# An embedding kernel's first image group: loaded and measured in two halves, weights scaled in between, GpSimd's table products held back

## The chip, the cores and the metric

The kernel runs on one core of a Trainium2 chip. The metric is the device time of one execution in microseconds (us); less is better. The engines of the core are called PE (matrix products), DVE (vector), ACT (scalar), POOL (GpSimd) and SP (the engine that here only issues transfers, "DMAs").

## The reference, cut to what matters

The model embeds 32 images and 32 texts and passes them through a scan layer and a mixture of experts. The change touches only the image embedding and, beside it, a set of tables for the scan layer:

```python
# x: (32, 3, 224, 224); P = 16, h = w = 14
x = transpose(x.reshape(B, C, h, P, w, P), (0, 2, 4, 3, 5, 1)).reshape(B, h*w, P*P*C)
x = layernorm(x, ln1_g, ln1_b)                 # over the 768 values of a patch
x = einsum('bnp,pd->bnd', x, W_proj) + b_proj  # 768 -> 192
x = layernorm(x, ln2_g, ln2_b)
x = concatenate([cls, x], axis=1) + pos_embedding
...
# scan layer: h = sigmoid(A) h + sigmoid(Bp) x_t,  y = sum over states of sigmoid(C) h
```

## The kernel before, in words

`embed_images` treats the 32 images as four groups of eight (`GB` = 8, `NGRP` = 4). One partition holds one row of patches of one image: 14 rows by 8 images make 112 partitions. `xg[g % 2]` is the tile of a whole group, [112, 48, 224]: 3 channels times 16 pixel rows (48), and 224 pixels. Two such tiles take turns, so groups 0 and 1 can be loaded at once, and groups 2 and 3 must wait until the tile is free. A group is worked on in 14 steps, one for each column of patches.

**The engines' parts.** DVE measures each patch (`x_stats`: two `bn_stats` of 384 values for a column, each over half of the 48 rows), then makes mean and deviation of all 14 columns (`x_moments`, `x_scales`, with one square root on ACT between them; the last one signals `x_rstd`). ACT normalises a column (`normalise`, signals `x_normed`). PE transposes it (`turn`) and multiplies it by the weights (`project`). DVE takes the product (`y_take`) and measures it for the second normalisation. PE may be two projections ahead of `y_take`, and ACT two columns ahead of PE. While DVE takes the products of group g it also measures group g+1 in the gaps; before the first `y_take` of group g it waits until group g+1 has arrived (`x_arrived(g + 1, 0)`).

**The weights.** The first normalisation's gain is multiplied into W_proj by DVE (six multiplications `wg<-wp,g`, six broadcasts `b1w<-b`, line 487 on); these wait for six loads issued by ACT (`w_in`), the last of them, `b<-in_L_tok_ln_b`, at 4.62 us. PE then makes the bias product `ps_b` (line 354).

**SP's list of transfers** is worked off in order, and each wait in it holds up all that stands behind it: group 0 (`whole(0)`, eight DMAs of 588 KB), the variable table's columns (`vt`, `vcol`, `vint`), the position embedding (`pos`, eight), `cls`, group 1 (`whole(1)`, eight DMAs), the store of the variable table, then `tables.store`, then groups 2 and 3 (line 221: 48 DMAs for each group), then the results' stores. `tables.store` (line 937) waits for POOL's tables to be done, stores three of them (`kd`, `lamd`, `c2d`), waits until they have landed, loads two back value by value (`lamc`, `c2c`, lines 945 and 946), and waits for these. Group 2's first piece also waits until eight columns of group 0 are normalised.

**POOL** makes constants and the scan layer's tables (`MixerTables.work`): `ex` is filled (line 1002), ACT takes its exponential, small products follow (lines 1005 to 1023), then the large products of `ex` (lines 1025 to 1031). After that POOL issues 64 indirect DMAs that gather the text features (lines 250 and 255); these are wanted only when the image stage is over.

Of the kernel before, what the change touches and what calls it, by code (L numbers as in the profile page):

```python
# [20 lines left out]
I32 = mybir.dt.int32  # L21
# [31 lines left out]
NF = 64  # L53
# [45 lines left out]
def embed_images(nc, io, dr, keep):  # L99

    with ExitStack() as ctx:
# [90 lines left out]
        @block.sync  # L192
        def _(sp):
            def whole(g):
                for b in BORDER:
                    sp.dma_start(xg[g][b:R:GB, :, :].rearrange("r (c p) w -> r c (p w)", c=CH),
                                 xv[g * GB + b].rearrange("h c p w -> h c (p w)")).then_inc(x_in[g % 2][0], 16)

            whole(0)
            sp.dma_start(vt[:, :, 0:NF], io["L0_txt_var_family_onehot"].rearrange("(p j) f -> p j f", p=128)  # L200
                          ).then_inc(tab, 16)
            for n, name in enumerate(["var_outer_norm", "var_inner_norm", "var_has_outer", "var_has_inner"]):
                sp.dma_start(vcol[:, n, :], io["L0_txt_" + name].rearrange("(p j) -> p j", p=128)).then_inc(tab, 16)
            for n, name in enumerate(["var_family_id", "var_group_id"]):
                sp.dma_start(vint[:, n, :], io["L0_txt_" + name].rearrange("(p j) -> p j", p=128)).then_inc(tab, 16)
            for b in BORDER:
                sp.dma_start(pos[b:R:GB, :, :].rearrange("r w d -> r (w d)"),
                             posv[0, 1:1 + NIMG, :].rearrange("(h w) d -> h (w d)", w=GRID)).then_inc(pos_in, 16)
            sp.dma_start(cls[:, 0, :], posv[0, 0, :].partition_broadcast(B)).then_inc(pos_in, 16)
            sp.dma_start(cls[:, 1, :], io["L0_tok_cls_token"][0, 0, :].partition_broadcast(B)).then_inc(pos_in, 16)  # L210
            whole(1)
            sp.wait_ge(tab, TAB_MADE)
            sp.dma_start(dr["var_tab"].rearrange("(p j) f -> p (j f)", p=128), vt[:].rearrange("p j f -> p (j f)")
                          ).then_inc(tab, 16)
            tables.store(sp)
            for g in range(2, NGRP):
                for n, (lo, hi) in enumerate(PIECES):
                    sp.wait_ge(x_normed, GRID * (g - 2) + hi)
                    for b in BORDER:
                        for c in range(CH):  # L220
                            sp.dma_start(xg[g % 2][b:R:GB, c * PATCH:(c + 1) * PATCH,
                                                   lo * PATCH:hi * PATCH],
                                         xv[g * GB + b][:, c, :, lo * PATCH:hi * PATCH]).then_inc(x_in[g % 2][n], 16)
            for g in range(NGRP):
                hi = GRID if g + 1 < NGRP else CUT
                sp.wait_ge(row_done, GRID * g + hi)
                store_rows(sp, h0, keep, g, 0, hi)

        @block.gpsimd
        def _(pool):  # L230
# [12 lines left out]
            pool.memset(zrow[:], 0.0).then_inc(misc, 1)  # L243
            tables.load(pool)
            tables.constants(pool)
            tables.work(pool)

            pool.wait_ge(ids, IDS_READY)
            for b in range(B):
# [76 lines left out]
        @block.tensor  # L326
        def _(pe):
            def turn(i, j):
                pe.wait_ge(x_normed, i + 1)
                pe.wait_ge(turned_out, i + 1)  # L330
                flat = xc[j][:, :, :].rearrange("r a q -> r (a q)")
                for k in range(KC):
                    t = pe.transpose(ps_t[j][k // 3][:, k % 3, :], flat[:, k * 128:(k + 1) * 128],  # L333
                                     keep["ident"][0:R, 0:R])
                t.then_inc(turned, 1)

            def project(i, j):
                pe.wait_ge(turned_out, i + 3)
                pe.wait_ge(y_taken, i + 1)
                for k in range(KC):  # L340
                    m = pe.matmul(ps_y[j][:], xt[j][:, k, :], wg[:, k, :], start=(k == 0), stop=(k == KC - 1))  # L341
                m.then_inc(projected, 1)

            pe.sem_inc(turned_out, 2)
            pe.sem_inc(y_taken, 2)
            pe.wait_ge(const, 7)
            pe.wait_ge(ids, IDS_FLOAT)
            for n in range(2):
                t = pe.transpose(ps_i[:, n, :], idf[:, n, :], keep["ident"][0:B, 0:B])
            t.then_inc(ids, 1)  # L350
            turn(0, 0)
            pe.wait_ge(w_ready, 1)
            for k in range(KC):
                m = pe.matmul(ps_b[:], b1w[:, k, :], wp[:, k % 2, k // 2, :], start=(k == 0), stop=(k == KC - 1))
            m.then_inc(bias_mm, 1)
            n = NGRP * GRID
            with pe.Fori(0, n // 2 - 1) as p:
                for j in range(2):
                    turn(2 * p + 1 + j, 1 - j)
                    project(2 * p + j, j)  # L360
            turn(n - 1, 1)
            project(n - 2, 0)
            project(n - 1, 1)

        @block.vector
        def _(dve):
# [5 lines left out]
                dve.wait_ge(step, done[0])  # L372

            def x_arrived(g, n):
                loads = sum(((n == 0) if i < 2 else CH) * GB for i in range(g % 2, g + 1, 2))
                dve.wait_ge(x_in[g % 2][n], 16 * loads)

            def x_stats(g, w):
# [95 lines left out]
            dve.wait_ge(ids, IDS_TURNED)  # L474
            dve.tensor_copy(keep["tid"][:], ps_i[:, 0, :]).then_inc(ids, 1)
            dve.tensor_copy(keep["vid"][:], ps_i[:, 1, :]).then_inc(ids, 1)
            x_arrived(0, 0)
            with dve.Fori(0, GRID // 7) as i:
                for a in range(7):
                    x_stats(0, 7 * i + a)  # L480
            x_moments(0)
            x_scales(0)
            dve.wait_ge(tab, COLS_IN)
            dve.tensor_copy(vt[:, :, NF:NF + 4], vcol[:].rearrange("p n j -> p j n")).then_inc(tab, 1)
            dve.tensor_copy(vt[:, :, NF + 4:NF + 6].bitcast(I32), vint[:].rearrange("p n j -> p j n")).then_inc(tab, 1)
            dve.wait_ge(w_in, 16 * W_LOADS)
            for k in range(KC):
                c, n = k // 2, k % 2
# [1 line left out]
                dve.tensor_copy(b1w[:, k, :], b1[:, n, c:c + 1].to_broadcast([128, R]))  # L490
            link(dve.memset(muy[:], 0.0))
            dve.sem_inc(w_ready, 1)
            dve.wait_ge(bias_mm, 1)
            link(dve.tensor_tensor(bias1[:], bias1[:], ps_b[:], ALU.add))
            for g in range(NGRP):
# [408 lines left out]
class MixerTables:  # L904
# [77 lines left out]
        act.wait_ge(self.argument, 1)  # L982
        act.activation(ex[:], ex[:], ACT.Exp).then_inc(self.powers, 1)

    def work(self, pool):
        abc, cw, lags, t1, c2, kr, ex, u3 = (self.abc, self.cw, self.lags, self.t1, self.c2, self.kr, self.ex, self.u3)
        a = abc[:, 0, :, :]
        done = [0]
# [2 lines left out]
        def link(ins):  # L991
            done[0] += 1
            ins.then_inc(self.step, 1)
            pool.wait_ge(self.step, done[0])
# [23 lines left out]
        for lag in range(3):  # L1018
            col = kr[:, :, HALO + Q - 1 - lag]
            link(tt(col, lags[:, lag, :, 0], cw[:, :, 3], ALU.mult))  # L1020
            for j in range(1, lag + 1):
                link(tt(u3[:], lags[:, lag - j, :, 0], cw[:, :, 3 - j], ALU.mult))
                link(tt(col, col, u3[:], ALU.add))
        pool.wait_ge(self.powers, 1)
        link(tt(ex[:].rearrange("p k n q -> p (k n) q"), ex[:].rearrange("p k n q -> p (k n) q"),
                c2[:].rearrange("p k n -> p (k n)").unsqueeze(2).to_broadcast([EB, NBLK * NS, Q]), ALU.mult))
        n = NS // 2
# [1308 lines left out]
```

## Time and profile before

| | us |
|---|---|
| median of 3 runs | 1362.22 (1362.19 to 1363.35) |
| the profiled execution, own time | 1361.33 |
| its span, first to last instruction | 1359.6 |
| PE busy | 1142.9 (84%) |
| DVE busy | 800.0 (59%) |
| ACT busy | 681.4 (50%) |
| POOL busy | 386.0 (28%) |
| image stage | 0 to 239.9 |

The profile records when each instruction of each engine started and how long it took, what ended the idle time before it, and what the DMA queues moved. The times in its rows count from the start of the span; the 1.7 us between span and own time lie outside of it. The image stage ends at 239.9 us, when the first instructions of the text stage start together on all engines; the change lies in the first 80 us of it.

### The profile page before, as it was taken

The page shows a single profiled execution, that of the slowest core. Times are in us where ns is not written, and L with a number is a line of the kernel's source. Part 1 is how long each engine was busy: PE and PEld are TensorE (multiplying, and loading weights), DVE is VectorE, ACT ScalarE, POOL GpSimd, SP SyncE. Part 2 cuts the span into 40 slices and gives each one's busy share as a digit, 9 for nine tenths or more (in the row PEclk, how much of TensorE's full clock was granted, in tenths as well). Part 3 has the DMA queues.
Part 4 walks back from the last instruction along what each step waited for, and adds up shares of the span by engine and source line. Part 5 has one row for each costly group of instructions (what it writes and reads, how often), then busy time and mean ns, then how long its engine had stood idle before and what let it go on. Part 6 is the DMA issues. An engine that isn't in the chain of part 4 may idle for free. (4 is left out here: it accounts for less than half of the span.)

```text
span 1359.6 us, 36429 instructions
## 1 busy us (share of the span) xinstructions
PE 1142.9 (84%) x11847; PEld 1084.0 (80%) x11847; DVE 800.0 (59%) x2533; ACT 681.4 (50%) x1524; POOL 386.0 (28%) x358
## 2 busy tenths in 40 slices
PE   0299994467479999999999499993999999999998
PEld 0298894244479899898997399992999999999998
DVE  0778878874732635536336377775456666656564
ACT  2165662255552333233233256562667777777775
POOL 5877100000200301103003025555123333333332
PEclk9999998676799999999999799996899999999999
DMA  8856412103511324234233789982111111111110
GB/s 187 192 93 143 123 37 54 41 0 99 243 28 28 81 83 100 61 100 104 64 95 75 225 267 297 288 250 84 29 42 47 47 42 43 47 43 44 47 44 21
DMA packets 166417, 133.72 MB, mean 98 GB/s; under 512 B 77989, under 2 KB 155932, under 8 KB 164704
## 3 DMA queue, kind: packets, MB, share of 16 engines
q1 hardware_dynamic: 152352, 112.22, 30.7%
q0 software_dynamic: 10384, 17.49, 4.1%
q10 hardware_dynamic: 3600, 3.01, 0.8%
q8 instruction: 41, 0.67, 0.2%
q14 instruction: 40, 0.33, 0.1%
HBM read 89.97 MB, written 43.53 MB: 98 GB/s over the span
## 5 line engine op out<-in xcount | busy, mean ns | idle before, releaser
L2116 POOL DMA_INDIRECT out_dram<-ob,oi x89 | 124.5, 1399 | 288.5 <-DVE ob L2170 283.0
L2226 PE MATMUL ph<-zt,wc 64*128 64x128 f32 x3204 | 198.3, 275 | 3.0 <-issue 1.5
L2226 PEld LDWEIGHTS ph<-zt,wc 64*128 64x128 f32 x3204 | 194.2, 191 | 4.4 <-issue 3.0
L2218 PE MATMUL py<-w2c,ht 64*128 64x192 f32 x2136 | 194.1, 327 | 2.3 <-DVE yb L2168 2.2
L1483 PE MATMUL pa<-wi,xn 96*85 96x96 f32 (+1 forms) x2048 | 185.5, 246 | 2.5 <-POOL mc L1335 2.5
L1483 PEld LDWEIGHTS pa<-wi,xn 96*85 96x85 f32 (+1 forms) x2048 | 180.4, 155 | 3.4 <-POOL mc L1335 2.8
L2141 ACT ACTIVATE ht<-ph,bc 128x128 f32<-128x128 f32 x534 | 156.5, 371 | 47.9 <-PE ph L2226 47.9
L2218 PEld LDWEIGHTS py<-w2c,ht 64*128 64x128 f32 x2136 | 172.6, 187 | 3.0 <-issue 1.7
L1346 POOL TENSOR_TENSOR bd<-rr,mc 128x656 f32<-128x656 f32 x48 | 61.6, 1282 | 289.8 <-PE pb L1501 171.2
L1357 DVE COPY x<-pa 85x384 f32<-85x384 f32 x100 | 55.4, 554 | 145.1 <-PE pa L1483 143.7
L341 PE MATMUL ps_y<-wg,xt 128*112 128x192 f32 x672 | 121.6, 332 | 14.0 <-DVE yg L431 14.0
L2135 ACT COPY w2c<-w2e 128x1152 f32 x89 | 102.6, 1152 | 60.6 <-PE py L2218 60.3
L341 PEld LDWEIGHTS ps_y<-wg,xt 128*112 128x112 f32 x672 | 108.9, 181 | 15.3 <-DVE yg L431 11.5
L1733 POOL DMA_INDIRECT xs<-row,sli x82 | 81.2, 990 | 98.5 <-issue 50.0
L1529 PEld LDWEIGHTS pa<-gp,x 85*128 85x128 f32 x768 | 92.1, 192 | 9.9 <-issue 3.8
L1529 PE MATMUL pa<-gp,x 85*128 85x128 f32 x768 | 93.0, 276 | 3.2 <-issue 3.2
L1376 ACT ACTIVATE yt<-pa 96x384 f32<-96x384 f32 (+1 forms) x84 | 44.6, 530 | 99.7 <-PE pa L1543 92.1
L1813 PE MATMUL p<-wo,y 128*128 128x192 f32 x492 | 92.8, 341 | 0.5 <-DVEq L1907 0.5
L333 PE MATMUL ps_t<-ident,xc 112*128 112x112 f32 x336 | 43.1, 266 | 53.9 <-ACT xc L281 53.9
L1813 PEld LDWEIGHTS p<-wo,y 128*128 128x128 f32 x492 | 82.4, 197 | 0.7 <-DVEq L1907 0.7
L333 PEld LDWEIGHTS ps_t<-ident,xc 112*128 112x128 f32 x336 | 38.8, 145 | 55.4 <-ACT xc L281 54.0
L2155 DVE TENSOR_SCALAR z<-xr 128x192 f32<-128x192 f32 x89 | 33.8, 379 | 68.8 <-DMA xr<-xs 68.8
(318 smaller groups left out, 1928.5 us busy)
## 6 DMA issues: line engine op xcount, KB each, us to landing
y<-yd SPq DMA_DIRECT2D x41, 384.0 KB, 4.0
gp<-kd SPq DMA_DIRECT2D x48, 246.0 KB, 2.8
xg<-in_x SPq DMA_DIRECT2D x16, 588.0 KB
xr<-xs SPq DMA_DIRECT2D x89, 98.0 KB, 1.9
yd<-yt SPq DMA_DIRECT2D x56, 144.0 KB, 1.9
hb<-h SPq DMA_DIRECT2D x41, 192.0 KB, 4.6
yd<-yt SPq DMA_DIRECT2D x40, 192.0 KB, 2.1
xg<-in_x SPq DMA_DIRECT2D x48, 112.0 KB
```

Source lines behind the costliest of these rows:

```text
L333: t = pe.transpose(ps_t[j][k // 3][:, k % 3, :], flat[:, k * 128:(k + 1) * 128], keep["ident"][0:R, 0:R])
L341: m = pe.matmul(ps_y[j][:], xt[j][:, k, :], wg[:, k, :], start=(k == 0), stop=(k == KC - 1))
L1346: pool.tensor_tensor(bd[g % 2][:], rr[g % 2][:, :].unsqueeze(1).to_broadcast([128, GE, Q]), mc[:, bass.ds(n, 1), :].rearrange("p a e -> p ...
L1483: mm = pe.matmul(p[:, i * EB:(i + 1) * EB], xn[0:rows, f, b, c * Q:c * Q + W], keep["wi"][0:rows, f, bass.ds(k * EB, EB)], start=(f == 0), ...
L1529: mm = pe.matmul(p[:, i, :], x[:, g * GE + e, :], cols(g % 3, e), start=True, stop=True)
L1733: pool.indirect_dma_start(dr["xs"], bass.IndirectOffsetOnAxis(ap=sli[j][:, t:t + 1], axis=0), row[j][:, t, :], None, bounds_check=bound, o ...
L1813: m = pe.matmul(po[q % 2][:, i, 0:D], yt[q][:, k, 1 - i, :], keep["wo"][:, k, :], start=(k == 0), stop=(k == KO - 1))
L2116: pool.indirect_dma_start(out, bass.IndirectOffsetOnAxis(ap=oi[j][:, 0:1], axis=0), ob[j][:], None, bounds_check=bound, oob_is_err=False). ...
L2135: act.copy(w2c[j % 2][:], w2[:, :, bass.ds(ex * D, D)]).then_inc(act_ok, 1)
L2141: act.activation(ht[j][:, c, :], ph[c % 4][:, c // 4, :], ACT.Gelu, bias=bc[j][:, c:c + 1]).then_inc(act_ok, 1)
L2218: m = pe.matmul(py[h][:], ht[j][r, k, :], w2c[j % 2][r, k, :], start=(k == 0), stop=(k == FC - 1))
L2226: return pe.matmul(ph[c % 4][:, c // 4, :], wc[j][r, f:f + 128], zt[j][r, part, :], start=start, stop=stop, skip_group_check=True)
```

## The change

Group 0's loads are issued in two rounds of eight: first pixel rows 0 to 7 of each patch row (the upper half of each patch, 294 KB for an image), then pixel rows 8 to 15. Each round has a semaphore of its own. DVE measures the upper halves of all 14 columns, then scales the weights, then measures the lower halves. The two copies into the variable table move behind the first group's moments, as before, but now come after the weights. On PE the first transposition moves behind the bias product. POOL waits for the first group's scales (`x_rstd`) before the large products. The counts of `x_arrived` follow the new loads. What is computed stays the same.

```diff
-            whole(0)
+            for n in range(2):
+                rows = slice(n * PATCH // 2, (n + 1) * PATCH // 2)
+                for b in BORDER:
+                    sp.dma_start(xg[0][b:R:GB, :, :].rearrange("r (c p) w -> r c p w", c=CH)[:, :, rows, :]
+                                 .rearrange("r c p w -> r c (p w)"),
+                                 xv[b][:, :, rows, :].rearrange("h c p w -> h c (p w)")).then_inc(x_in[0][n], 16)
...
-            tables.work(pool)
+            tables.work(pool, x_rstd)
...
-            turn(0, 0)
             pe.wait_ge(w_ready, 1)
             for k in range(KC):
                 m = pe.matmul(ps_b[:], b1w[:, k, :], wp[:, k % 2, k // 2, :], start=(k == 0), stop=(k == KC - 1))
             m.then_inc(bias_mm, 1)
+            turn(0, 0)
...
-                loads = sum(((n == 0) if i < 2 else CH) * GB for i in range(g % 2, g + 1, 2))
+                loads = sum((1 if i == 0 else (n == 0) if i == 1 else CH) * GB for i in range(g % 2, g + 1, 2))
...
-            x_arrived(0, 0)
-            with dve.Fori(0, GRID // 7) as i:
-                for a in range(7):
-                    x_stats(0, 7 * i + a)
-            x_moments(0)
-            x_scales(0)
-            dve.wait_ge(tab, COLS_IN)
-            dve.tensor_copy(vt[:, :, NF:NF + 4], vcol[:].rearrange("p n j -> p j n")).then_inc(tab, 1)
-            dve.tensor_copy(vt[:, :, NF + 4:NF + 6].bitcast(I32), vint[:].rearrange("p n j -> p j n")).then_inc(tab, 1)
+            def first_stats(n):
+                x_arrived(0, n)
+                rows = slice(n * PATCH // 2, (n + 1) * PATCH // 2)
+                for w in range(GRID):
+                    dve.bn_stats(st[:, w, n, :], xg[0][:, :, w * PATCH:(w + 1) * PATCH]
+                                 .rearrange("r (c p) q -> r c p q", c=CH)[:, :, rows, :])
+
+            first_stats(0)
             dve.wait_ge(w_in, 16 * W_LOADS)
             for k in range(KC):
...
             link(dve.memset(muy[:], 0.0))
             dve.sem_inc(w_ready, 1)
+            first_stats(1)
+            x_moments(0)
+            x_scales(0)
+            dve.wait_ge(tab, COLS_IN)
+            dve.tensor_copy(vt[:, :, NF:NF + 4], vcol[:].rearrange("p n j -> p j n")).then_inc(tab, 1)
+            dve.tensor_copy(vt[:, :, NF + 4:NF + 6].bitcast(I32), vint[:].rearrange("p n j -> p j n")).then_inc(tab, 1)
             dve.wait_ge(bias_mm, 1)
...
-    def work(self, pool):
+    def work(self, pool, first_scales):
...
         pool.wait_ge(self.powers, 1)
+        pool.wait_ge(first_scales, 1)
         link(tt(ex[:].rearrange("p k n q -> p (k n) q"), ex[:].rearrange("p k n q -> p (k n) q"),
                 c2[:].rearrange("p k n -> p (k n)").unsqueeze(2).to_broadcast([EB, NBLK * NS, Q]), ALU.mult))
```

## Rows read from the trace of the kernel before

**Rows 1.** DVE's timeline: start us, duration us, engine, line, operation, count, [idle before <-releaser]
```profile
32.86 12.97 DVE L381 BATCH_NORM_STATS2 st<-xg  x28 [27.98 <-DMA xg<-in_x]
...
46.28 4.78 DVE L391 TENSOR_SCALAR mx<-mx 112x14 f32<-112x14 f32 x1
...
57.17 0.17 DVE L403 SCALAR_TENSOR_TENSOR nb<-mx,rs 112x14 f32<-112x14 f32 x1
...
57.43 0.32 DVE L489 TENSOR_SCALAR wg<-wp,g 128x192 f32<-128x192 f32 x1
...
64.09 0.35 DVE L494 TENSOR_TENSOR bias<-bias,ps_b 112x192 f32<-112x192 f32 x1 [4.33 <-PE ps_b L354]
66.95 0.36 DVE L431 TENSOR_TENSOR yg<-ps_y,bias 112x192 f32<-112x192 f32 x1 [2.51 <-PE ps_y L341]
```

**Rows 2.** DVE's timeline, the first product taken in each of two later stretches
```profile
120.97 0.36 DVE L431 TENSOR_TENSOR yg<-ps_y,bias 112x192 f32 x1 [3.31 <-DMA xg<-in_x]
...
161.60 0.36 DVE L431 TENSOR_TENSOR yg<-ps_y,bias 112x192 f32 x1 [2.68 <-DMA xg<-in_x]
```

**Rows 3.** SP's timeline from 76 us on
```profile
77.29 82.25 SPq L221 DMA_DIRECT2D xg<-in_x  x96
```

**Rows 4.** SP's timeline up to 76 us
```profile
0.81 7.09 SPq L196 DMA_DIRECT2D xg<-in_x  x8
...
8.62 17.97 SPq L203 DMA_DIRECT2D vcol<-in_L_txt_var_outer_norm  x1
...
38.01 7.29 SPq L196 DMA_DIRECT2D xg<-in_x  x8
...
57.97 0.42 SPq L940 DMA_DIRECT2D kd<-kr  x1
...
59.02 0.54 SPq L942 DMA_DIRECT2D c2d<-c  x1
...
68.42 3.50 SPq L946 DMA_DIRECT2D c2c<-c2d  x1
```

**Rows 5.** Waits of SP's queue: line <- waited for: us in total, times, longest
```profile
SPq L945 <- DMA c2d<-c: 8.4, 1, 8.4
...
SPq L221 <- DMA c2c<-c2d: 0.4, 1, 0.4
```

**Rows 6.** ACT's timeline: the eighth column of group 0 normalised
```profile
75.78 1.04 ACT L281 ACTIVATE xc<-xg,nb,rs 112x768 f32 x1
```

**Rows 7.** Windows: stretch, us, busy us of five engines (instructions), PE clock, DMA share, GB/s
```profile
64.00:66.00 2.00, 2.00 (x15) 2.00 (x14) 0.35 (x1) 1.00 (x3) 1.39 (x3) 1.00 0.83 235
66.00:68.00 2.00, 2.00 (x17) 1.98 (x16) 1.05 (x3) 1.17 (x3) 1.70 (x2) 1.00 0.38 46
```

**Rows 8.** DMA issues: out<-in, queue, count, KB each, median us from issue to landing
```profile
yd<-yt SPq DMA_DIRECT2D x40, 192.0 KB, 2.1
...
b<-in_L_tok_ln_b ACTq DMA_DIRECT2D x1, 84.0 KB, 28.5
```

**Rows 9.** DMA queues, 18 to 22 us (q1 is SP's, q10 ACT's): packets, MB, share of 16 engines
```profile
q1 hardware_dynamic: 72, 0.72, 81.4%
q10 hardware_dynamic: 72, 0.00, 1.7%
```

**Rows 10.** DVE's timeline: group 2's moments, the first and the last instruction
```profile
135.76 0.07 DVE L388 MEMSET d<- 112x14 f32 x1
...
138.07 0.17 DVE L403 SCALAR_TENSOR_TENSOR nb<-mx,rs 112x14 f32<-112x14 f32 x1
```

**Rows 11.** POOL's timeline: the large products and the last gather
```profile
36.27 8.97 POOL L1025 TENSOR_TENSOR ex<-ex,c 96x5248 f32<-96x5248 f32 x1
45.32 10.43 POOL L1029 TENSOR_TENSOR ex<-ex 96x2624 f32<-96x2624 f32 x3
55.83 0.75 POOL L1031 TENSOR_TENSOR kr<-ex 96x328 f32<-96x328 f32 x1
...
140.19 0.95 POOL L255 DMA_INDIRECT vr<-var_tab,vid  x1 [0.30 <-issue]
```

## The prediction, made before the changed kernel was run

> **What bounds the kernel now.** I read the page's slices first and then only the first 240 us, since all edits lie in the image stage and the stages behind it start when it ends. The question is therefore what sets that end. DVE's timeline answers it backwards: twice DVE has nothing to take because a group of images has not come, 3.31 us before 120.97 and 2.68 us before 161.60 [rows 2]. Both instants hang on SP: from 77.29 on it issues the 96 loads of groups 2 and 3 without a gap, 82.25 us, so 0.857 us each, until 159.54 [rows 3]. The second group's 48 end at 77.29 + 41.1 = 118.4, the third's at 159.5, and DVE goes on 2.5 and 2.1 us later. So the stage's end is tied to the start of these issues: whatever happens before, the time moves as 77.29 moves.
>
> What sets 77.29? SP works its list in order. Its waits say that it stood for c2d's landing, 8.4 us behind the issue that ended at 59.56, so until 67.98 [rows 4, 5]; then it issued the two value-by-value loads, and the wait named last ahead of the 96 is again on one of them, c2c [rows 5]. From 67.98 to 77.29 is 9.3 us. A second condition is nearly as late: eight columns of group 0 normalised, at 75.78 + 1.04 = 76.82 [rows 6]. Gaining needs both earlier.
>
> And 67.98? The tables were ready at 55.83 + 0.75 = 56.58 [rows 11] and issued from 57.97 on [rows 4], but they stand behind group 1's eight loads, 4.8 MB, issued from 38.01 on. The windows show the queue moving 235 GB/s up to 66 us and 46 after that [rows 7]. Group 1's transfer, not the tables, sets c2d's landing, and the tables had slack. Group 1 in turn was issued late because SP stood 17.97 us at one 4 KB load of the variable table, until 26.6 [rows 4], while group 0 filled the queues; 11.4 us of other issues follow before 38.01.
>
> **The first scales (`x_rstd`).** Before: group 0 is there at 32.86, the 28 measurements take 12.97 us (0.463 each), and the moments last until 57.34 [rows 1], 11.5 us. Undisturbed moments take 2.5 us, 135.76 to 138.24 [rows 10]. The difference is POOL: a multiplication of 14 values took 4.78 us [rows 1] while POOL's sums of `ex` ran [rows 11]. Holding POOL back removes 9.0 us there. The split removes half of the measurements from behind the arrival: 14 x 0.463 = 6.5 us.
>
> Against that stands the weights' scaling, 57.43 to 59.76 (64.09 less its 4.33 idle), 2.3 us [rows 1], now ahead of the lower half. It is hidden only if its loads come early. The last of them landed 28.5 us after its issue at 4.62, at 33.1 [rows 8], as late as the images. The two queues were served packet for packet: 72 and 72 in the same 4 us [rows 9]. Halving the image packets gives ACT's queue twice the turns, but its long small loads also need them; between "right after the upper half's measurements" (hidden, 0) and "with the last image packet" (all 2.3 on the path) I take the second, as 33.1 and 32.86 lie together.
>
> The Trainium skill says otherwise on the turns: "DMA: Bandwidth & Descriptors", section "Queues, rings and completion order", has an engine drain a whole packet of several descriptors from one ring before it switches. By that the weights could land anywhere in the lower half's load, the 2.3 us would be hidden, and the tables' term below would come out 2.3 us less, with the sum unchanged by the queue's term and the chance of the small-loss end greater. The equal counts speak against the rule here.
>
> So `x_rstd` comes at 33.4 + 2.3 + 6.5 + 2.5 = 44.7 (33.4: 32.86 with 0.5 for small loads that now fall into the image load), 12.6 us earlier than 57.34.
>
> **The tables.** POOL's large products take 36.27 to 56.58, 20.3 us [rows 11], and start at 44.8 instead: done at 65.1, 8.5 us later. kd and c2d are then issued; c2d's issue starts 1.05 us behind kd's [rows 4], and a store of this size lands 2.1 us after its issue in an empty queue [rows 8]. That gives 65.1 + 0.1 + 1.05 + 2.1 = 68.4, and up to 70.5 if the weights or the lower half are 2 us later. So the slack that POOL's tables had is used up: +0.4, from 0 to +2.5.
>
> **The queue's term.** Eight more issues at 0.89 us (7.09 / 8) end at 15 instead of 7.9 [rows 4]; hidden, because SP then stood until 26.6 anyway. What ends that stand the trace does not say; it ended 6.2 us before group 0 landed. If time or bytes decide, it ends as before, and group 1 with it: 0. If the number of packets still in the queue decides, it now ends half as far before the landing, as the packets are half as long: 3.1 us later, and everything behind it in SP's list shifts by 3.1. That SP then went on to 38.01 without another such stand speaks for a queue that had run down, so I take 2.2, nearer the upper end. c2d lands at 67.98 + 2.2 = 70.2, which is later than the tables' 68.4 and hides it.
>
> **The other parts.** Two copies to the variable table now meet POOL's first large product; if one of them waits as the multiplication in [rows 1] did, it lasts up to 8.97 us, to 54; its store then is issued ahead of the old 57.5 and still behind group 1: nothing. Without that cover it would cost up to 8.97. On PE the bias product (4.33 us of DVE's wait in [rows 1]) runs at 36 to 41 while PE has nothing else, so the first projection is ready at about 50 instead of 66.9. But DVE's first `y_take` waits for group 1, which landed at 65 to 66 [rows 7] and now at 67 to 68: of 16 us nothing is left. PE is two projections ahead then, which saves 1.9 us up to the eighth column: 67.5 + 9.9 - 1.9 = 75.5, earlier than c2c. POOL's 64 gathers start 8.5 us later and end at 149.7 instead of 141.1 [rows 11]; they are wanted at 239.9. Once the 96 issues run, the waits at 120.97 and 161.60 only move with them.
>
> **The sum.** Group 2's first issue: 70.2 + 9.3 = 79.5, 2.2 us later. The profiled execution's own 1361.33 becomes 1363.5; the median of the runs lies 0.9 above it, 1362.2, so the prediction is 1364.4. What this kernel's measurement can tell from no change is about 0.2%, 2.7 us.
>
> **Rivals.**
> (a) *Slower by the same mechanism at its full size or beyond.* SP's stand ends 3.1 us later or more, or the lower half lands a few us late, which delays both terms. From a shift of 2.7 on it counts as slower; at 3.1 the time is 1365.3, and 2 us more of image load make it 1367.3. For it: two terms that each reach +2.5 to +3.1 and only the larger counts. Against it: equal bytes, and the tables alone cost 0.4. Chance 0.37.
> (b) *A small gain.* The stand ends early, since ACT's queue empties faster. Then group 1 follows group 0 directly, c2d hangs on the tables alone, and at best (weights hidden) that is 68.4 - 2.3 = 66.1: 1.9 us earlier, 1360.3. Inside the bound, part of the "same" chance, 0.15.
> (c) *The early gain survives.* The halved packets load quicker, group 1 starts with group 0's end some 10 us earlier, and both conditions for 77.29 move with it: 1352. It needs a group to load much quicker than in the 32 us from its first issue at 0.81 to 32.86 [rows 1, 4], which equal bytes do not suggest. Chance 0.08 with all gains over 2.7.
> (d) *Halved DMAs load much slower.* If each added load cost what a load alone shows, 2.1 us [rows 8], and nothing of it overlapped, eight of them would delay the lower half by 16.8 us and the sum to 1379 or more. But the 112 KB loads of [rows 3] follow each other at 0.857 us, less than that. Chance 0.02, counted with (a). The Trainium skill's "DMA: Bandwidth & Descriptors", section "Bandwidth", speaks for it: it asks for DMAs of 1 MiB or more, and by the fit in its "Anatomy of one DMA" (2 us plus bytes by 436 GB/s) sixteen separate halves would take 43 us against 27 for eight whole loads, an estimate from that page; no run so far shows such loads one at a time.
>
> **The numbers.** The forecast, group 2's start 0 to 2.7 us later, has 0.40; with (b)'s 0.15 that is 0.55 for "same"; slower 0.37, faster 0.08. The forecast's own range is 1362.2 to 1364.9; the 8-in-10 range leaves out most of (c) and (d) and the far end of (a): 1361.0 to 1367.4.
>
> **What would show it.** Right: large products starting at about 45; moments of about 2.5 us; SP's list standing until 27 to 30; DVE's first `y_take` at 65 to 68, waiting on a DMA; line 221 from 77 to 81 on, still 82 us long, and waits for `xg` of 3 us or more in the same two places. Wrong: group 1 loaded before 62, the 96 issues starting before 75, or no wait for `xg` at 120 and 160; and, on the other side, the lower half landing after 36 or the two copies holding up SP's list.

## The result and the profile after

In the first comparison the changed kernel took 1356.79 us in the median of 6 runs (1354.03 to 1363.36), the kernel before 1362.98 in 6 runs: ratio 0.9953 (changed to before), 95% interval 0.9937 to 0.9970. That is faster by 0.47%, and the time lies below the predicted range. It did not come back at that size. Two more comparisons gave 1359.91 (11 runs; ratio 0.999, 0.9978 to 1.0002) and 1360.71 (12 runs; 0.9988, 0.9974 to 1.0001); neither of these two is clear of no change by itself. Over all runs of the three comparisons, and of one more in which before ran, the medians are 1359.47 (29 runs of the changed kernel) and 1361.80 (74 of before), the means 1359.72 and 1361.50. So the change is worth about 2 us, some 0.15%. One kernel's own runs spread over 13 us (before: 1354.53 to 1367.30).

DVE's timeline of the changed kernel (columns as in [rows 1]; "..." stands for rows left out) shows the early half of the story:

```profile
20.02 6.53 DVE L486 BATCH_NORM_STATS2 st<-xg 112x6 f32<-112x384 f32 x14 [15.94 <-DMA xg<-in_x]
26.47 0.30 DVE L493 TENSOR_SCALAR wg<-wp,g 128x192 f32<-128x192 f32 x1
...
28.88 0.07 DVE L495 MEMSET muy<- 112x14 f32 x1
31.63 6.53 DVE L486 BATCH_NORM_STATS2 st<-xg 112x6 f32<-112x384 f32 x14 [2.68 <-DMA xg<-in_x]
38.12 0.07 DVE L393 MEMSET d<- 112x14 f32 x1
...
40.39 0.17 DVE L408 SCALAR_TENSOR_TENSOR nb<-mx,rs 112x14 f32<-112x14 f32 x1
...
40.65 0.34 DVE L504 TENSOR_TENSOR bias<-bias,ps_b 112x192 f32<-112x192 f32 x1
65.08 0.36 DVE L436 TENSOR_TENSOR yg<-ps_y,bias 112x192 f32<-112x192 f32 x1 [24.09 <-DMA xg<-in_x]
```

The weights fit into the gap between the halves without a wait of their own, the moments take 2.4 us, and `x_rstd` comes at 40.6 instead of 57.3 [rows 1]: 16.8 us earlier. The last line takes nearly all of it back: DVE stands 24.09 us for group 1, and the first product is taken at 65.08 instead of 66.95. SP's timeline and its waits (SPq and POOLq are the queues of SP's and POOL's instructions) tell why nothing more follows:

```profile
0.81 13.91 SPq L202 DMA_DIRECT2D xg<-in_x  x16
...
15.44 10.46 SPq L208 DMA_DIRECT2D vcol<-in_L_txt_var_outer_norm  x1
25.95 0.42 SPq L208 DMA_DIRECT2D vcol<-in_L_txt_var_inner_norm  x1
...
36.81 6.87 SPq L196 DMA_DIRECT2D xg<-in_x  x8
...
61.07 0.33 SPq L950 DMA_DIRECT2D kd<-kr  x1
...
66.35 0.39 SPq L955 DMA_DIRECT2D lamc<-lamd  x1
...
75.80 82.25 SPq L226 DMA_DIRECT2D xg<-in_x  x96
```

```profile
SPq L950 <- POOLq L1043: 16.8, 1, 16.8
SPq L223 <- ACT xc L286: 4.6, 1, 4.6
SPq L955 <- DMA c2d<-c: 3.8, 1, 3.8
SPq L226 <- DMA c2c<-c2d: 0.8, 1, 0.8
```

SP's stand at the small load ends at 25.9, against 26.6 before [rows 4]; group 1 goes out 1.2 us earlier; the tables, which had slack before, are now waited for by SP itself (16.8 us for POOL); c2d has landed at 66.35 instead of 67.98; and the 96 loads start at 75.80 instead of 77.29 [rows 3]. Their 82.25 us are unchanged to the second decimal. The two conditions for their start are still nearly tied: the eighth column, at 73.86 + 1.04 = 74.90 on ACT, then c2c, 0.8 us behind.

```profile
73.86 1.04 ACT L286 ACTIVATE xc<-xg,nb,rs 112x768 f32 x1
```

POOL's timeline has the products where `x_rstd` puts them, done at 60.99:

```profile
40.73 8.97 POOL L1036 TENSOR_TENSOR ex<-ex,c 96x5248 f32<-96x5248 f32 x1 [6.91 <-DVE nb L408]
49.78 10.38 POOL L1040 TENSOR_TENSOR ex<-ex 96x2624 f32<-96x2624 f32 x3
60.24 0.75 POOL L1042 TENSOR_TENSOR kr<-ex 96x328 f32<-96x328 f32 x1
```

So the image stage gained 1.5 us at the start of the 96 loads, and 1.2 at its end. The profiled execution itself took 1363.36 us, 2.0 more than the one profiled before: what came behind the image stage was 3.2 us longer in it. Whether that belongs to the change is the first question of the experiments.

### The profile page after: what moved, and what is told of

Its sections match the earlier page's. It is cut to its first block and busy times, and to the rows that moved or that the text cites. A ratio compares the mean times of both kernels' runs of the same rounds, so it can differ in the third digit from the quotient of the medians.

```text
span 1361.6 us, 36390 instructions
## 1 busy us (share of the span) xinstructions
PE 1147.1 (84%) x11847; PEld 1085.4 (80%) x11847; DVE 790.5 (58%) x2533; ACT 681.3 (50%) x1524; POOL 388.8 (29%) x358
## 5 line engine op out<-in xcount | busy, mean ns | idle before, releaser
L346 PE MATMUL ps_y<-wg,xt 128*112 128x192 f32 x672 | 125.8, 340 | 28.8 <-DVE yg L436 28.8
L346 PEld LDWEIGHTS ps_y<-wg,xt 128*112 128x112 f32 x672 | 112.4, 185 | 30.8 <-DVE yg L436 26.5
L1744 POOL DMA_INDIRECT xs<-row,sli x82 | 82.2, 1002 | 99.5 <-issue 50.5
L2189 DVE COPY wc<-w1e 128x1152 f32 x89 | 67.7, 760 | 0.0
L2218 PE MATMUL pz<-ident,z 64*128 64x64 f32 x712 | 51.2, 261 | 15.9 <-DVE z L2168 15.9
```

The source lines that it names most:

```text
L1744: pool.indirect_dma_start(dr["xs"], bass.IndirectOffsetOnAxis(ap=sli[j][:, t:t + 1], axis=0), row[j][:, t, :], None, bounds_check=bound, o ...
L2189: dve.tensor_copy(wc[j][:], w1[:, bass.ds(ex * WE, WE)]).then_inc(wc_ok, 1)
L2218: t = pe.matmul(pz[:, h, k, :], z[j][r, k * KT:(k + 1) * KT], ident[r, r], start=True, stop=True, skip_group_check=True)
```

## The experiments

For each profiled execution: the first product taken by DVE, the first of the 96 loads, the start of the text stage (SP's first load for it), the span, and the rest, which is the span less the text stage's start (us). "The hold" is POOL's wait for the first scales; "both moves" are the two calls moved on SP, explained below.

| kernel | first product | 96 loads | text stage | span | rest |
|---|---|---|---|---|---|
| before | 66.95 | 77.29 | 239.90 | 1359.6 | 1119.7 |
| before, again | 65.74 | 76.42 | 239.57 | 1361.2 | 1121.6 |
| changed | 65.08 | 75.80 | 238.66 | 1361.6 | 1122.9 |
| changed, again | 64.99 | 75.97 | 238.57 | 1358.2 | 1119.6 |
| changed, third | 64.27 | 75.63 | 236.88 | 1358.9 | 1122.0 |
| before, hold only | 76.78 | 86.75 | 249.49 | 1369.3 | 1119.8 |
| changed, no hold | 65.53 | 76.33 | 239.01 | 1357.1 | 1118.1 |
| changed, stores late | 66.45 | 76.37 | 238.63 | 1355.4 | 1116.8 |
| changed, group 1 early | 59.17 | 74.94 | 237.74 | 1355.0 | 1117.3 |
| changed, both moves | 59.48 | 69.75 | 231.80 | 1345.3 | 1113.5 |
| before, both moves | 66.19 | 76.09 | 239.31 | 1353.8 | 1114.5 |
| both moves, group 0 whole | 61.21 | 68.70 | 233.51 | 1347.1 | 1113.6 |
| both moves, columns first | 53.71 | 61.20 | 224.10 | 1342.9 | 1118.8 |
| both moves, columns last | 59.95 | 69.83 | 232.17 | 1348.7 | 1116.5 |

Two things stand in it already. From the first of the 96 loads to the text stage it is 161.3 to 164.8 us in all fourteen, while that start itself moves over 25 us. And the rest differs by up to 9.4 us between executions with the same code behind the image stage, by 3.3 us among the three of the changed kernel alone. The part of it that varies most is the last stage, from PE's first product `ph<-zt,wc` to the end: 402.7 to 407.7 us. The seven kernels with a moved call have the shorter rests (1113.5 to 1118.8, against 1118.1 to 1122.9 without one). Whether the moves shorten it or this is chance was not tested, so what a move is worth is read from the image stage.

**The two kernels again** (no edit). The question was whether the first result's 6 us lie in the image stage.

> The changed kernel once more, to get a second trace of it. Theory A (all of the change lies in the image stage, and the stages behind it take the same time): the 96 loads of groups 2 and 3 begin at 75.8 us as in the first trace, 1.5 us earlier than before, the text stage begins at 238.7, and the runs lie within 2 us of 1361. Theory B (most of the 6 us lies behind the image stage and differs from execution to execution): the image stage ends at 238.7 again, but the span is 3 to 9 us shorter than the 1361.6 of the first trace, and one later stage, most likely the experts' (from 937 us on), holds the difference.

> The kernel before once more, for a second trace of it. Theory A: image stage to 239.9 us, mixer from 387.9, experts from 947, all within 0.5 us. Theory B: the image stage within 0.5 us, the experts' stage differing by several us from the first trace.

Measured: the changed kernel 1359.91, ratio 0.999 (0.9978 to 1.0002), one run of before 1362.9. Theory A holds for what repeats, B for what was seen once: the changed kernel's markers of the image stage came back within 0.2 us, those of before 0.3 to 1.2 us earlier, and the other 4.5 us of the first result did not come back.

**The hold alone.** The kernel before, with POOL waiting for the first scales ahead of its large products; group 0 is loaded and measured as before, and the weights are scaled behind the moments.

```diff
-            tables.work(pool)
+            tables.work(pool, x_rstd)
...
         pool.wait_ge(self.powers, 1)
+        pool.wait_ge(first_scales, 1)
```

> The kernel before with POOL's large products held until the first group's scales, and nothing else changed. By the path that I read (tables' stores, then the two value-by-value loads, then the 96 loads): scales at 45.8 + 2.5 = 48.3, tables done at 68.7, the stores landed at about 72, the 96 loads from 81.4 instead of 77.3: the text stage begins 4 us later, at 244, and the time is 4 us longer if nothing else differs (1366 to 1367). A rival, by which holding POOL back is what brings the gain: text stage at 236 or earlier.

Measured: 1371.59, ratio 1.0073 (1.0057 to 1.0088), so 10 us slower, far more than the 4 expected. DVE's timeline and POOL's:

```profile
49.28 9.03 DVE L489 TENSOR_SCALAR wg<-wp,g 128x192 f32<-128x192 f32 x1
...
58.36 5.76 DVE L489 TENSOR_SCALAR wg<-wp,g 128x192 f32<-128x192 f32 x1
...
64.17 3.00 DVE L489 TENSOR_SCALAR wg<-wp,g 128x192 f32<-128x192 f32 x1
...
76.78 0.36 DVE L431 TENSOR_TENSOR yg<-ps_y,bias 112x192 f32<-112x192 f32 x1 [2.26 <-PE ps_y L341]
```

```profile
49.00 9.19 POOL L1026 TENSOR_TENSOR ex<-ex,c 96x5248 f32<-96x5248 f32 x1 [12.21 <-DVE nb L403]
58.27 10.44 POOL L1030 TENSOR_TENSOR ex<-ex 96x2624 f32<-96x2624 f32 x3
```

A weight multiplication that takes 0.31 us (0.30 in the changed kernel above) ends at 58.31, when POOL's first product ends at 58.19; the next wait for POOL's next products. The moments got free and the weights took their place under the products, with the bias product and all of PE behind them. In the changed kernel the weights are done before POOL is released, so this never meets.

The Trainium skill has this in "SBUF — State Buffer", section "Who interferes with whom": DVE and GpSimd share a pair of ports, taken for a whole instruction, and `tensor_scalar` is among the operations that can want it. The ends in these rows agree with that.

**The change without the hold.**

```diff
-        pool.wait_ge(first_scales, 1)
```

> The changed kernel without POOL's wait for the scales. By the path that I read the hold brings nothing here: POOL's large products begin at about 34 and end at 54, the moments are stretched by them to about 53, and yet the first product is still taken at 65, when group 1 has landed, and the 96 loads begin at 75 to 76: text stage at 238.7, within 0.7 us. The rival, by which the hold matters: moments at 53 delay the first products and the text stage begins at 240 or later.

Measured: 1360.45, ratio 0.9988 (0.9967 to 1.0008). The moments last until 54.0 under POOL's products, 13.5 us longer, and the start of the 96 loads does not show it:

```profile
38.87 3.82 DVE L396 TENSOR_SCALAR mx<-mx 112x14 f32<-112x14 f32 x1
...
42.98 5.59 DVE L399 TENSOR_TENSOR dev<-dev 112x56 f32<-112x56 f32 x1
...
65.53 0.36 DVE L436 TENSOR_TENSOR yg<-ps_y,bias 112x192 f32<-112x192 f32 x1 [11.07 <-DMA xg<-in_x]
```

DVE still waits 11.07 us for group 1, and the loads start at 76.33, behind c2c. The hold is worth nothing here, and 13.5 us of earlier scales are worth nothing.

**What swallows the gain: two calls moved on SP.** First each alone in the changed kernel, then both, then both in the kernel before.

```diff
             for n, name in enumerate(["var_family_id", "var_group_id"]):
...
+            whole(1)
             for b in BORDER:
...
-            whole(1)
             sp.wait_ge(tab, TAB_MADE)
...
-            tables.store(sp)
             for g in range(2, NGRP):
...
+            tables.store(sp)
```

> The changed kernel with one call moved on SP: the stores of the tables, with their waits, stand behind the 96 loads of groups 2 and 3 instead of ahead of them. Theory T (SP's list ties the stage's end to the tables; the second condition, the eighth column normalised, is nearly as late): the 96 loads start when the eighth column of group 0 is normalised, 65.1 + about 8 to 10 = 73 to 75 instead of 75.8; the text stage at 236 to 238 instead of 238.7, so 1 to 3 us less than the changed kernel, 1357 to 1359. Rival U (the list is not what binds; something else in the early stage sets 75.8): 75.8 and 238.7 stay.

Measured: 1357.2, ratio 0.9977 (0.9961 to 0.9993). But the loads start at 76.37, not 73 to 75, and the text stage at 238.63, as in the changed kernel. In SP's timeline and waits the tables are gone and the other condition stands at the same place:

```profile
76.37 82.23 SPq L225 DMA_DIRECT2D xg<-in_x  x96
```

```profile
SPq L225 <- ACT xc L286: 31.6, 2, 31.2
```

Between the first product and the loads lie 9.92 us, 0.8 less than in the changed kernel (65.08 to 75.80); in the kernel before it was 9.87 up to the eighth column [rows 1, 6]. Theory T's tie was right, its earlier start was not: the first product came at 66.45 in this execution, not at 65.1, and the 9.92 us lie at the far end of its 8 to 10. The lower time of this kernel's runs is not in its image stage.

> The changed kernel with one call moved on SP: group 1's eight loads are issued ahead of the position embedding and the cls row. Theory T (the early gain of DVE is lost first in the wait for group 1, then in SP's list): group 1 comes 5 to 10 us earlier, the first product is taken at 55 to 60 instead of 65.1, but the 96 loads still start at 73 to 76, since the large products end at 61 and the three stores, their landing, and the two value-by-value loads take about 14 us behind that; 0 to 2.5 us less than the changed kernel. Rival U (group 1 alone binds): the 96 loads start as much earlier as the first product is, 5 to 8 us, and the text stage with them.

Measured: 1358.35, ratio 0.9981 (0.9965 to 0.9998). The first product is taken 5.9 us earlier, the loads start 0.9 us earlier, now behind c2c alone. DVE then stands at the next station:

```profile
74.94 82.28 SPq L226 DMA_DIRECT2D xg<-in_x  x96
```

```profile
SPq L226 <- DMA c2c<-c2d: 5.2, 1, 5.2
```

```profile
118.66 0.36 DVE L436 TENSOR_TENSOR yg<-ps_y,bias 112x192 f32 x1 [8.93 <-DMA xg<-in_x]
```

Before it was 3.31 us there [rows 2]. That is theory T; rival U is out.

> The changed kernel with both calls moved on SP: group 1 ahead of the position embedding, the stores of the tables behind groups 2 and 3. Theory T: both covers are off, so the early gain of the scales reaches the loads: first product at 55 to 60, the 96 loads from 65 to 69, the text stage at 228 to 232, 6 to 10 us less than the changed kernel, 1350 to 1354, and still waits for groups 2 and 3. Rival U (the loads of groups 2 and 3 are not what sets the stage's end once they are early): the waits for xg at 120 and 160 vanish and the text stage comes only 3 us earlier.

Measured: 1351.87, ratio 0.9928 (0.9902 to 0.9955). The loads start at 69.75 (65 to 69 was expected), 6.05 us earlier than in the changed kernel, and the text stage at 231.80, 6.9 earlier. Neither move alone gave more than 1 us in the image stage; together they give the gain.

```profile
59.48 0.36 DVE L436 TENSOR_TENSOR yg<-ps_y,bias 112x192 f32<-112x192 f32 x1 [18.20 <-DMA xg<-in_x]
```

```profile
69.75 82.26 SPq L225 DMA_DIRECT2D xg<-in_x  x96
```

```profile
SPq L225 <- ACT xc L286: 25.8, 2, 25.4
```

> The kernel before with the same two calls moved on SP. Theory T: here the weights, the bias product and the late scales hold the first product at about 66.9, whatever group 1 does, and the eighth column at about 76; the 96 loads start at 76 to 77 instead of 77.3, the text stage at 238.5 to 240, 0 to 1.5 us less than before. The difference to the changed kernel with both moves, 7 to 11 us, is then what the halved first group, the early weights and the held products are worth once nothing swallows it. Rival U: both kernels with the moves take the same time within 2 us.

Measured: 1359.09, ratio 0.9997 (0.9981 to 1.0013). With the same two moves the kernel before starts the loads at 76.09 and gains nothing: its first product comes at 66.19, behind 2.17 us of wait on PE, as it did without the moves (2.51 us, [rows 1]), so an earlier group 1 can give it nothing.

```profile
66.19 0.36 DVE L431 TENSOR_TENSOR yg<-ps_y,bias 112x192 f32<-112x192 f32 x1 [2.17 <-PE ps_y L341]
```

```profile
76.09 82.26 SPq L220 DMA_DIRECT2D xg<-in_x  x96
```

The difference between the two kernels with the moves is 7.5 us at the text stage and 7.2 in the medians. That is what the change is worth when its cover is off; with the cover it is the 1 to 2 us measured.

**The changed kernel a third time** (no edit), beside the next three.

> The changed kernel once more, on another chip, beside the same runs of before as the three kernels below. Theory A (what the change moves is the start of the 96 loads, by 0.7 to 1.5 us, and the rest of the first result is spread between executions): 0.5 to 3 us less than before, 96 loads at 75.5 to 76.5, text stage at 238.2 to 239.2. Theory B (the change itself is worth the first result's 6 us): 5 to 7 us less.

Measured: 1360.71, ratio 0.9988 (0.9974 to 1.0001). Theory A; the text stage came at 236.88, 1.3 us earlier than expected.

**Whole loads again.** Both moves, the changed order on DVE and the hold, but group 0 in eight loads; DVE waits once for all of group 0, and its counts follow (not shown).

```diff
-            for n in range(2):
-                rows = slice(n * PATCH // 2, (n + 1) * PATCH // 2)
-                for b in BORDER:
...
+            whole(0)
```

> The changed kernel with both moves on SP, but group 0 loaded in whole patches again, eight loads; the upper halves are still measured first, then the weights scaled, then the lower halves, and the products held. So the loading in halves alone is undone. Theory T (only group 1's arrival and SP's list matter, and the scales have 18 us of slack): the upper halves start at about 32, the scales come at 49 to 51 instead of 40.6, and yet the first product is at 59 to 60 and the 96 loads at 69 to 70: the same time as with both moves, within 1.5 us; the halves are worth nothing. Rival U (the halves carry the gain): first product and 96 loads 6 to 9 us later, 1358 to 1361.

Measured: 1351.84, ratio 0.9941 (0.9921 to 0.9960). The scales come at 50.5 and DVE still waits 10.28 us for group 1:

```profile
61.21 0.36 DVE L431 TENSOR_TENSOR yg<-ps_y,bias 112x192 f32<-112x192 f32 x1 [10.28 <-DMA xg<-in_x]
```

The loads start at 68.70, no later than with halves, though the first product comes 1.7 us later: the eighth column follows it by 7.5 us here and by 10.2 with halves (the last section tells why). The text stage came 1.7 us later all the same. The difference lies behind the last wait for images (DVE goes on at 154.23, with halves at 154.20), a stretch that takes 76.9 to 79.3 us over the fourteen profiles; the medians are equal. The halves by themselves gave no measurable gain; what counts of the change is that weights, bias product and moments are out of the way by about 59.

**What SP's stand hangs on: the columns first, the columns last.** With both moves, the seven loads of the variable table (one of 256 KB, six of 4 KB) ahead of group 0, or behind group 1. SP's stand at the second of them, the first of 4 KB, was the queue's term of the prediction.

Columns first:

```diff
+            sp.dma_start(vt[:, :, 0:NF], io["L0_txt_var_family_onehot"].rearrange("(p j) f -> p j f", p=128)
+                          ).then_inc(tab, 16)
...
             for n in range(2):
                 rows = slice(n * PATCH // 2, (n + 1) * PATCH // 2)
...
-            sp.dma_start(vt[:, :, 0:NF], io["L0_txt_var_family_onehot"].rearrange("(p j) f -> p j f", p=128)
-                          ).then_inc(tab, 16)
...
             whole(1)
```

Columns last:

```diff
+            whole(1)
             sp.dma_start(vt[:, :, 0:NF], io["L0_txt_var_family_onehot"].rearrange("(p j) f -> p j f", p=128)
                           ).then_inc(tab, 16)
...
-            whole(1)
```

> The changed kernel with both moves, and the seven loads for the variable table (vt, vcol, vint) issued ahead of group 0. It asks what SP's stand of 10.5 us at the first vcol load hangs on. Theory Q (on what stands ahead of it in the queue): no stand, the seven loads take 0.4 to 0.7 us each, group 0 is issued from 4.3 to 18.2, group 1 directly behind it (or stands there in its place, at some load of group 1, until about 26); if group 1 follows directly, its issue ends near 26 instead of 36.4 and it lands at 48 to 56 instead of 58.4, the 96 loads start 3 to 10 us earlier, 1342 to 1349. Theory C (the load of single values itself stands long, or until a fixed time): the stand is then ahead of group 0, which lands at 42 or later, and the time is 1355 or more.

> The changed kernel with both moves, and group 1's eight loads issued directly behind group 0, ahead of the seven loads for the variable table. Theory Q: group 1 is issued from 14.8 to 22, perhaps with a stand at one of its loads; the stand at vcol then comes behind group 1 and ends 15 to 25 us later than 26. Group 1 lands at 48 to 56. The copies into the table wait for these columns on DVE, ahead of the first product: it comes at 50 to 58, the 96 loads at 60 to 68, 1341 to 1350. Theory C (a fixed time ends the stand): SP goes on at 26 as before.

SP's timeline, columns first:

```profile
1.59 0.63 SPq L202 DMA_DIRECT2D vcol<-in_L_txt_var_outer_norm  x1
...
4.63 13.84 SPq L208 DMA_DIRECT2D xg<-in_x  x16
18.51 6.78 SPq L196 DMA_DIRECT2D xg<-in_x  x8
...
61.20 82.28 SPq L225 DMA_DIRECT2D xg<-in_x  x96
```

and columns last:

```profile
14.78 6.78 SPq L196 DMA_DIRECT2D xg<-in_x  x8
...
22.27 27.22 SPq L209 DMA_DIRECT2D vcol<-in_L_txt_var_outer_norm  x1
...
69.83 82.27 SPq L225 DMA_DIRECT2D xg<-in_x  x96
```

and DVE's row for the copies, columns last:

```profile
58.39 1.09 DVE L501 COPY vt<-vcol 128x32 f32<-128x32 f32 x1 [18.55 <-DMA vint<-in_L_txt_var_group_id]
```

First: 1346.31, ratio 0.9877 (0.9847 to 0.9908), the fastest kernel of this study, 15.7 us below before. The stand is gone, group 1 follows group 0 directly, the first product comes at 53.71 and the text stage at 224.10, 15.8 us earlier than before. DVE's later waits for images have shrunk to one of 1.00 us there, so the 96 loads have little left to give. Last: 1353.54, ratio 0.9943 (0.9925 to 0.9960); the stand grew to 27.22 us, ended at 49.5, and the columns came so late that DVE's copies stood 18.55 us for them, so that of the early group 1 nothing was left; theory Q's time for it (1341 to 1350) was missed by that. The same 4 KB load takes 0.63 us ahead of the images, 10.46 behind one group and 27.22 behind two. Theory Q; a fixed time (theory C) is out. The number of image packets is out too: with group 0 whole, half as many packets, the stand ended at 26.4, with halves at 25.9. What fits is the amount of data ahead: the second group's 4.8 MB (eight of 588 KB) put the end off by 23.6 us; at the 195 to 231 GB/s that the windows of that execution show from 20 to 50 us they need 21 to 25. What makes just this load stand was not separated: group 1's eight image loads behind the same 4.8 MB took 6.78 us and did not stand, and the 256 KB load of `vt` is directly ahead of the 4 KB load in every run.

## Why the prediction was wrong, point by point

**The bound: right.** The stage's end follows the start of the 96 loads in fourteen profiles, by 161.3 to 164.8 us, and that start is set by two conditions nearly tied. Moving one of them gave nothing (76.37) or little (74.94), moving both gave 69.75. Of the two waits for `xg` forecast at 3 us or more, the second was 1.95 us (at 160.19), the first 4.81 (at 119.52).

**`x_rstd`: right in kind, 4.1 us too late** (44.7 forecast, 40.6 measured). The halves' 6.5 and the moments' 2.5 came as costed (6.53 and 2.44). The lower half landed at 31.6, not at 33.4, and the weights' 2.3 us were hidden: the last of their loads landed 20.9 us after its issue instead of 28.5 [rows 8]. The prediction had named this end (twice the turns for ACT's queue; 72 became 133) and taken the other. The queues' rows at 18 to 22 us of the changed kernel, half as long packets, still nearly one for one:

```profile
q1 hardware_dynamic: 145, 0.75, 74.2%
q10 hardware_dynamic: 133, 0.10, 15.0%
```

The Trainium skill's rule of a whole packet per ring before a switch ("DMA: Bandwidth & Descriptors", section "Queues, rings and completion order") would have given the right outcome, weights hidden. The counts do not show it as the reason, nor do they speak against it, as the prediction had it: how many descriptors a counted packet holds no run shows.

**The tables' term.** 61.0 instead of 65.1 for POOL, by the same 4 us, and c2d landed at 66.35 instead of 68.4. The landing took 4.4 us from its issue at 61.96, against the 2.1 taken, while group 1 was still arriving (until 65.08); with group 1 early c2d was issued at 62.61 and SP went on at 65.69, after 3.1, and with both moves, behind all image loads, at 153.15 and 155.52, after 2.4.

**The queue's term: the step that failed.** "I take 2.2, nearer the upper end": SP's stand did not end later but at 25.90, 25.75 and 25.39 in three profiles, against 26.59 and 25.66. Its price is 0 or a little below. It was booked by number of packets; the last experiments rule that out and fit the data ahead, which the change leaves as it was. "If time or bytes decide, it ends as before" was in the text as the other end.

**The sum.** With 0 for the queue and the tables 2 us earlier, the 96 loads start at 75.8, not at 79.5: -1.5 instead of +2.2. The forecast of 1364.4 becomes 1360.7; 29 runs have 1359.47. This is rival (b), a small gain with c2d at 66.1 and 1360.3 us, which had a chance of 0.15. Its reason (group 1 directly behind group 0) did not happen, and that its numbers did is in part luck: POOL was done 1.8 us earlier than (b) took it with the weights hidden (61.0 for 62.8), and the landing was 2.3 us longer (4.4 for 2.1), so that two errors cancel. The 1356.79 of the first comparison lies another 4 us below this sum, and no step of the prediction accounts for them ("the first 6 us" below).

**The saving on PE** (1.9 us up to the eighth column) did not come: 65.08 to 74.90 is 9.8 us, before 66.95 to 76.82 is 9.9. It did come, at 2.4 us, in the three kernels in which PE's granted clock was 1.00 at the first product; at 0.50 the projection that starts there takes 2 us longer (table in the last section). The prediction had no term for the clock.

**The first 6 us.** They are not a property of the change that repeats. The three profiles of the changed kernel start the text stage at 238.0 in the mean, the two of before at 239.7: 1.7 us, and the means over all runs differ by 1.8. Behind the image stage the changed kernel took 1119.6 to 1122.9, before 1119.7 and 1121.6. The prediction's bound of 0.2% was read from three runs that happened to lie within 1.2 us; 74 runs of the same kernel lie within 13. Why the interval of the first comparison, 0.9937 to 0.9970, does not hold what the later two gave stays open: spread behind the image stage is enough in size, but what makes it was not found. The two later comparisons ran on two chips; on which the first ran is not on record, so a difference between chips is not excluded.

**Rivals.** (a) did not happen, since its two terms were 0 and less. (c) did not, as it stood: group 0's lower half landed at 31.6 and group 1 went out at 36.8. That the two moves gave its 1352, and the columns first 1346, is no confirmation: those are other edits. (d) is out: 16 halved loads follow each other at 0.87 us and land together as early as eight whole ones (31.6 against 32.9, and 31.7 in the second profile of before). The fit that the prediction cites for it is stated in the Trainium skill ("DMA: Bandwidth & Descriptors", section "Anatomy of one DMA") for DMAs that GpSimd issues; these are issued by SP.

## What to carry to other kernels

Seventeen us gained at one engine were worth about 2, because two waits behind it were due at the same time as before: follow the gain to the next wait, and to the one tied with it, and free both before judging the change. A list of transfers worked off in order is a chain of its own: SP stood at a 4 KB load behind 4.8 MB, and everything behind it stood too; with the table's seven loads moved to the front the same load took 0.63 us, and the text stage came 7.7 us earlier than with the two moves alone. If one engine's work is held back to free a shared resource, ask what runs on the other when it is released: the hold alone cost 10 us.

## What the runs showed of the hardware

The issue of a DMA can itself stand for the data queued ahead: 0.63, 10.46 and 27.22 us for the same 4 KB load, while the next one of 4 KB takes 0.42 or 0.43. Not every load does: eight image loads behind the same 4.8 MB took 6.78 us together.

PE's granted clock fell to 0.50 in the changed kernel; in the kernel before the profile has 1.00 from 36 to 70 us ([rows 7] has 64 to 68). The windows of the changed kernel (columns as in [rows 7]):

```profile
38.00:46.00 8.00, 4.32 (x18) 4.09 (x19) 2.48 (x15) 5.07 (x9) 5.27 (x1) 0.50 0.90 209
46.00:50.00 4.00, 4.00 (x28) 3.93 (x28) 0.00 (x0) 2.09 (x4) 3.92 (x2) 0.95 0.87 197
54.00:60.00 6.00, 0.00 (x0) 0.00 (x0) 0.00 (x0) 0.00 (x0) 5.84 (x3) 0.50 0.89 201
66.00:70.00 4.00, 4.00 (x15) 3.81 (x14) 4.00 (x11) 0.00 (x0) 2.85 (x3) 0.50 0.59 6
```

and of the kernel before:

```profile
60.00:66.00 6.00, 6.00 (x26) 5.76 (x27) 0.35 (x1) 2.58 (x6) 4.47 (x6) 1.00 0.85 202
```

0.50 is the level of 1.2 GHz. PE had stood idle from 33.1 to 41.7, after the bias product, and again from 50.5 to 65.5, and was at the lower level when it went on. Twelve products of a projection took 3.38 us at 44.00, in the 0.50 stretch, and 2.12 at 47.79, at 0.95. The column alone can mislead: in the kernel before the twelve products of the bias, of the same size, took 4.18 us at 59.87 under a granted clock of 1.00, after PE had stood idle for 54 us and turned one column (1.38 us). It is safer to read the duration beside it.

The first of these stretches is hidden behind the wait for group 1. The second is not. At the first product PE starts its third projection, and the eighth column follows sooner or later with the clock that PE then has:

| kernel | PE idle before its third projection | granted clock then | third projection | first product to eighth column |
|---|---|---|---|---|
| changed | 15.01 | 0.50 | 4.18 | 9.82 |
| both moves | 8.24 | 0.50 | 4.18 | 10.24 |
| both moves, columns last | 11.04 | 0.50 | 4.18 | 9.86 |
| changed, no hold | 1.51 | 1.00 | 2.20 | 7.47 |
| both moves, group 0 whole | 0.89 | 1.00 | 2.21 | 7.46 |
| both moves, columns first | 1.66 | 1.00 | 2.20 | 7.46 |

So about 2 of the 2.4 to 2.8 us that the first three lose lie in that one projection. The third execution of the changed kernel and the one with group 1 early lie between: 4.00 and 3.61 us for the projection, 9.27 and 8.87 up to the eighth column. PE stood longest where its work ahead was done long before group 1 came, and there the lower clock took back what its head start should have given.
